# A decoder-layer kernel: one PSUM bank taken from the spread of B and given to the common set

## What is computed

```python
x = x + attn(layernorm(x))            # 16 heads of 32; chunked linear attention with feature maps, rms norm per head
x = x + mixer(ctx, layernorm(x))      # selective scan over 512 steps, 512 channels, 16 states; gate silu(z)
x = x + ffn(layernorm(x))             # 512 -> 2048 gate and value, ternary weights, 8-bit activations, -> 512

# mixer, the part that the change touches
dA = exp(d[..., None] * A)
state = state * dA + (d * u)[..., None] * b[:, None, :]
y = einsum('bdn,bn->bd', state, c)
```

## Time and profile before

| | us |
|---|---|
| median of 3 runs (lowest, highest) | 1216.23 (1215.35, 1216.56) |
| the profiled execution, its own time | 1215.45 |
| its span, first to last instruction | 1213.7 |
| busy: TensorE / VectorE / ScalarE / GpSimd | 893.5 / 928.2 / 585.0 / 435.6 |
| mean granted TensorE clock | 0.821 of full |

### The profile page before, as it was taken

One profiled execution on the slowest core, in us unless ns is written; L12 is line 12 of the kernel. 1 busy time (PEld: TensorE's weight loads), 2 busy tenths in 40 slices (PEclk: granted clock), 3 DMA queues, 4 the chain that ended last, 5 costly groups with the idle time before them and its releaser, 6 DMA issues.

```text
span 1213.7 us, 11854 instructions
## 1 busy us (share of the span) xinstructions
PE 893.5 (74%) x3970; PEld 487.3 (40%) x3970; DVE 928.2 (76%) x1065; ACT 585.0 (48%) x887; POOL 435.6 (36%) x264
## 2 busy tenths in 40 slices
PE   4576765636628989978628989978628999976597
PEld 1334333414222346555222446555222356743233
DVE  4878889999897676888798676988798668853453
ACT  2787426345435763453435763454435754321332
POOL 0134554344345332534245332534245334540100
PEclk8688686655958999985958999985958999967699
DMA  9368778776535533646335533646335435740000
GB/s 323 109 185 237 171 191 227 176 190 188 115 81 120 124 76 72 159 91 154 82 79 121 122 77 71 158 95 153 82 80 112 114 87 130 168 93 0 1 9 26
DMA packets 57120, 147.20 MB, mean 121 GB/s; under 512 B 7938, under 2 KB 8322, under 8 KB 57060
## 3 DMA queue, kind: packets, MB, share of 16 engines
q0 software_dynamic: 18432, 67.12, 28.8%
q1 hardware_dynamic: 38628, 79.32, 20.9%
HBM read 74.96 MB, written 4.35 MB: 65 GB/s over the span
## 4 chain that ended last, share of the span: by engine, by line
PE 43%; DVE 27%; DMA 14%; issue 7%; ACT 6%; POOL 1%; SPq 0%; DVEq 0%; POOLq 0%; ACTq 0%
PE bank L586 16%; DMA ACC<-W 14%; PE bank L750 7%; DVE W L1381 7%; PE bank L615 4%; DVE W L1372 4%; PE bank L766 3%; PE bank L665 3%; PE bank L634 3%; PE bank L747 2%; PE bank L686 2%; DVE BST L1308 2%; DVE U L1331 2%; DVE X L1529 1%; POOL W L1235 1%
## 5 line engine op out<-in xcount | busy, mean ns | idle before, releaser
L1235 POOL TENSOR_TENSOR W<-W,CROW 128x1024 f32<-128x1024 f32 x128 | 310.7, 2427 | 473.4 <-DVE W L1381 473.3
L1381 DVE TENSOR_TENSOR_SCAN W<-DEC,W 128x1024 f32<-128x1024 f32 x122 | 306.3, 2511 | 0.1
L1243 POOL DMA_DIRECT2D ACC<-W x128 | 115.0, 898 | 178.5 <-DMA ACC<-W 152.6
L1372 DVE TENSOR_TENSOR W<-DU,PB 128x1024 f32<-128x1024 f32 x128 | 153.1, 1196 | 21.5 <-PE PB L712 11.3
L948 ACT ACTIVATE DEC<-DT,ACOL 128x511 f32<-128x511 f32 x244 | 160.0, 712 | 5.7 <-DVE W L1381 5.6
L750 PE MATMUL bank<-W,ARENA 128*128 128x512 fp8e4 x512 | 144.1, 408 | 0.0
L615 PE MATMUL bank<-IDF,ARENA 128*128 128x128 f32 x400 | 64.8, 311 | 82.5 <-DVE ARENA L1549 53.3
L895 ACT ACTIVATE ARENA<-bank 128x512 f32<-128x512 f32 x56 | 33.1, 592 | 157.4 <-PE bank L634 80.2
L1470 DVE SCALAR_TENSOR_TENSOR ARENA<-bank,SDQ,ARENA 128x512 f32<-128x512 f32 x64 | 47.6, 747 | 79.3 <-PE bank L750 50.8
L615 PEld LDWEIGHTS bank<-IDF,ARENA 128*128 128x128 f32 x400 | 54.4, 162 | 104.8 <-issue 90.0
L1019 ACT ACTIVATE ARENA<-bank,SDQ 128x512 f32<-128x512 f32 x64 | 43.5, 685 | 80.4 <-PE bank L750 80.3
(11 more groups left out here) (158 smaller groups left out, 1466.3 us busy)
## 6 DMA issues: line engine op xcount, KB each, us to landing
ACC<-W POOLq DMA_DIRECT2D x128, 512.0 KB, 5.6
CROW<-c_rows SPq DMA_DIRECT2D x128, 256.0 KB, 3.5
W<-in_wffn SPq DMA_DIRECT2D x27, 512.0 KB, 7.2
X<-in_wffn SPq DMA_DIRECT2D x21, 512.0 KB, 5.7
X<-in_x SPq DMA_DIRECT2D x7, 1024.0 KB, 9.3
out_dram<-X SPq DMA_DIRECT2D x16, 256.0 KB, 2.1
X<-in_ctxT SPq DMA_DIRECT2D x4, 512.0 KB, 4.7
ARENA<-in_x SPq DMA_DIRECT2D x1, 1024.0 KB, 5.6
```

The costliest lines, as they stand in the source:

```text
L1235: pool.tensor_tensor(w, w, CROW[u % 2][:, :].unsqueeze(1).broadcast_to([P, 2, L]), ALU.mult)\
L1243: pool.dma_start(ACC[accumulator(u)][:, :, :], w, accum_op=ALU.add).then_inc(y_summed.sem, 16)
L1372: dve.tensor_tensor(W[u % 4][:, :, :], DU[:, 2 * h:2 * h + 2, :], PB[u % 3][:, :].unsqueeze(1).broadcast_to([P, 2, L]), ALU.mult)\
L1381: dve.tensor_tensor_scan(w, flat(decay_of(u)), w, 0.0, ALU.mult, ALU.add).then_inc(scan_done.sem, 1)
```

## The change

One bank moves from PB to the common set; PSUM's eight banks are all in use before and after. The diff, cut to its core:

```diff
-    every, four, last = (0, 1, 2, 3, 4), (0, 1, 2, 3), (4,)
+    every, five, last = (0, 1, 2, 3, 4, 5), (0, 1, 2, 3, 4), (5,)
...
-        return [(key, last if key[1] == "o" else four) for key in attention_products(b)]
+        return [(key, last if key[1] == "o" else five) for key in attention_products(b)]
...
-        out += on((0, 1, 4) if b < BATCH else every, [(f, "yT", t) for t in range(TT)])
+        out += on((0, 1, 4, 5) if b < BATCH else every, [(f, "yT", t) for t in range(TT)])
...
-        R = Banks(ctx, nc, "bank", 5, all_products())
-        PB = [ctx.enter_context(nc.psum_tensor(f"PB{i}", [P, 512], fp32)) for i in range(3)]
+        R = Banks(ctx, nc, "bank", 6, all_products())
+        PB = [ctx.enter_context(nc.psum_tensor(f"PB{i}", [P, 512], fp32)) for i in range(2)]
...
-                if u >= 3:
-                    pe.wait_ge(*dbu_done.at(0, u - 2))
+                if u >= 2:
+                    pe.wait_ge(*dbu_done.at(0, u - 1))
...
-                pe.matmul(PB[u % 3][:, :], ID96[:, n:n + 1].broadcast_to([96, P]), BC3[b % 2][:, :],
+                pe.matmul(PB[u % 2][:, :], ID96[:, n:n + 1].broadcast_to([96, P]), BC3[b % 2][:, :],
...
-                                  PB[u % 3][:, :].unsqueeze(1).broadcast_to([P, 2, L]), ALU.mult)\
+                                  PB[u % 2][:, :].unsqueeze(1).broadcast_to([P, 2, L]), ALU.mult)\
```

More of the change, by code:

```diff
@@ L171, in attention @@
     def attention(b):
-        return [(key, last if key[1] == "o" else four) for key in attention_products(b)]
+        return [(key, last if key[1] == "o" else five) for key in attention_products(b)]
     out = on(every, front_products(0) + [(0, "dt", e) for e in range(KT)] + [(0, "xnT", k) for k in range(KT)])
-    out += on(four, [(0, "q", 0), (0, "k", 0), (0, "v", 0)] + front_products(1))
+    out += on(five, [(0, "q", 0), (0, "k", 0), (0, "v", 0)] + front_products(1))
     out += attention(0)
@@ L178, in all_products @@
         f = b - 1
-        out += on(four, [(f, "ms", GROUPS - 1)])
+        out += on(five, [(f, "ms", GROUPS - 1)])
         if b < BATCH:
-            out += on(four, [(b, "dt", 2), (b, "dt", 3)] + [(b, "xnT", k) for k in range(KT)])
+            out += on(five, [(b, "dt", 2), (b, "dt", 3)] + [(b, "xnT", k) for k in range(KT)])
         out += on(every, [(f, "wo", t) for t in range(TT)])
@@ L191, in all_products @@
         if b < BATCH:
-            out += on(four, [(b, "v", 0)])
+            out += on(five, [(b, "v", 0)])
         out += on(every, [(f, "O", TT - 1)])
```

## The result

The changed kernel is slower. Its median is **1221.48 us** (11 runs, 1217.73 to 1224.42) against 1215.78 us (11 runs, 1212.93 to 1218.05) for the kernel before on the same chip. The ratio is 1.0046, 95% interval 1.0033 to 1.0059: 5.6 us by the ratio, 5.7 by the medians. The profiled execution took 1222.39 us, its span is 1220.6 us, 6.9 more than that of before, its mean granted clock 0.822.

A forecast was written before the change was run, and what follows sets the result against it. No engine bounds the kernel alone (chain: TensorE 43%, VectorE 27%, accumulating DMA 14%). Terms 1.3 + 0 + 2.1 + 0.2 = +3.6 us on the profiled 1215.45 give 1219.05, plus 0.78 for the median: 1219.8, range 1215.3 to 1227.0.

The forecast's parts named there:

- Place 1: Row 0's start: the spread of unit 2 waits for `inputs_b(0)` and delays q; +1.3 us (0.6 to 1.9).
- Place 2: Row 0's attention: unit 17's spread runs 5.0 us later, covered by VectorE's 3.66 us DMA wait; 0 (0 to 2.7).
- the worse of its two cases: Row 0's attention, group 1: k as slow as before, VectorE 4.2 us late; at full clock 1.6 us.
- Place 3: Three feed-forwards beside units: the clock falls after the new stop; +0.7 us each, +2.1 in all (-1.2 to +6.6).
- Place 4: Last attention group of rows 1 and 2: unit 63's spread waits some 4 us; +0.2 us for both (0 to 1.0).
- Gained, 0: Bank waits elsewhere than in the feed-forward are 1 us or less, or end in a data wait: nothing gained.
- Not slower: the stops are free: Row 0's start costs 0.6 us, TensorE keeps full clock in the feed-forward: -0.6 us, about 1215.6 to 1217; chance 0.25.
- More half clock: Row 0's start, feed-forwards and last attention groups at their upper ends: +9.5 us, 1225.7; chance 0.20.
- Faster: the freed bank wins outright: Feed-forward without bank wait or clock fall: hT 5.4 us earlier, three times 16.2, 1201.3; chance 0.05.

The follow-up runs named there:

- the first experiment: The kernel before with two spread banks instead of three, the common set kept at five and the eighth bank unused: 1223.82 us, ratio 1.0068.
- the one with both moves: The changed kernel with unit 2's spread issued behind q and k, and three spreads of each feed-forward beside units issued later: 1204.80 us, ratio 0.9921.

## Why the prediction was right, and where its terms were off

The forecast was +3.6 us and 1219.8; the medians give +5.7 and 1221.48, inside the range, slower as the likeliest case. The mechanism holds: the tighter wait costs time where TensorE is on the path, through TensorE's clock, and most of it has cover. The terms don't all hold, and that the sum came this near is in part luck:

- **The reading of the earlier trace rows was wrong.** "19 of 128 spreads, 27.2 us in all" counts weight loads and matmuls of the same spreads. It was 13 spreads, and 10.5 us of stops between matmuls. The conclusion drawn from it, that a tighter limit bites there, stands; no term of the sum uses the figure.
- **Place 1, +1.3 (0.6 to 1.9): too small in the profiled execution, right in others.** The later start of q was as worked out, 1.9 us. What failed in the profiled execution is "if the clock rises at the same moment as before, part of the slow stretch is spent waiting". The clock rose later too: 0.58 in 55 to 60 where before had 0.98, q took 6.50 us. 2.7 us at conv, above the upper end. In three other kernels with two banks and the start as in after, whose executions began otherwise, the step held, and the loss at conv was 0.7 to 1.3 us. Nor does all of it last: of after's delay 1.1 us was left when the first feed-forward began.
- **Place 2, 0 (0 to 2.7): right.** The k product was slow (5.92 us), as in the worse of its two cases; VectorE came 5.8 us late to the scores, 3.1 of them new (4.2 were worked out, where its own numbers give 4.1), and left the group 2.4 us late, less than the 2.7 that it had come with. The wait of 3.66 us for the DMA was the cover and is gone.
- **Place 3, +0.7 each, +2.1 in all: too small.** Measured +1.8, +2.1 and +2.0, 5.9 in all, near the upper end of +2.2 each. The step that failed is that I took the new stop before the second spread for the one that brings the clock down. The stop before the first spread, 2.70 us, already did. Four to five products at 2.35 us followed, and not two or three. The second stop, worked out as 3.1 us, was then 0.74. The added matmuls show that the clock is the price: with the waits kept and the clock full the same stretch is 1.0 to 1.3 us quicker than before.
- The Trainium skill's rule that I weighed there ("TensorE: Matmul & The Clock Gate", section "A second HAM failure mode: psum-queue depth-cycling") pointed the right way: the granted clock was 0.50 and 0.52 in the thirteen microseconds behind 381 where before had 1.00 and 0.64, and filling the stop held it at 1.00. Of the upper ends that I had tied to it, this place came near its own and place 1 went past it at conv; places 2 and 4 stayed low.
- **Place 4, +0.2: right.** The transposes behind the last spread of row 1's attention are still released by VectorE's `feature` step, after a wait of 0.36 us (554.91). From the end of one feed-forward to the start of the next VectorE's delay even fell, by 0.5 us over row 1, 0.6 over row 2 and 2.4 over row 3. There the half clock lies elsewhere, as one window of the last groups of row 3's attention shows (0.81 and 1.00), of before and then of after:

```profile
1060.00:1080.00 20.00, 15.68 (x97) 10.84 (x96) 16.14 (x15) 6.81 (x11) 10.62 (x7) 0.81 0.61 122
```

```profile
1060.00:1080.00 20.00, 17.70 (x113) 11.81 (x114) 15.41 (x17) 8.34 (x14) 10.18 (x7) 1.00 0.62 132
```

- **Gained, 0: not settled.** The waits for banks other than the earlier trace rows were read as "1 us or less, or end in a wait for data". One of them is 1.50 us, before "xin" 3, and it went. The freed bank by itself gave some 2.7 us by the ratios of after and of the first experiment, within their intervals. Against it stand the two slow xdbl, 5.3 us and not 3.6, on the path: +1.7 and +2.0 us, which no term has. That the freed bank makes them slow is not shown: with "xin" 3 held back both stay slow, and with five banks the one of row 1 is slow as well.
- VectorE's delay in the profiled execution adds up as follows: 1.1 when the first feed-forward began, 5.9 in the three steps, 4.0 at the ends of the three feed-forwards (1.7, 2.0, 0.4), less 3.4 between them, and 0.5 in the last part: +8.1. The prediction had 1.3 for the first, 2.1 for the second, nothing for the ends and +0.2 for what lies between. What it missed at the ends and what came back between them nearly cancel, and nothing in it foresaw either.

**The rivals.** "Not slower: the stops are free" fell; its point was whether matmuls behind the stop take 1.3 us a product, and they took 2.35. "More half clock" is what happened in the feed-forward; its sum of +9.5 was not reached, in the profiled execution because of the time that came back between the feed-forwards. "Faster: the freed bank wins outright" did not happen, but its mechanism and price are real: 5.4 us a feed-forward were worked out, and -4.8 to -5.1 measured in before with other placements, -4.0 to -4.9 in the changed kernel with the spreads moved and V placed. What kept it from happening is what the prediction named, `inputs_b` of the unit before, and a second thing that it had not seen: V had no bank either.

## What to carry to other kernels

A buffer taken from an in-order queue's most frequent product costs little in waiting (88 us more of stops here, and almost all covered) and more in what the waiting does to TensorE's clock: look at what the granted clock is behind each new stop and price the products after it at that level. A wait for a bank is a statement on one product and the one that stood in its bank: before adding a bank at another's cost, look at whom it waits for and put it where something is drained early; here three placements gave 12 us, where the extra bank alone gave some 2.7 within the noise, and 5.6 once the spreads were out of its way. A total that a view gives for a line can hold a weight load and its matmul: look at them apart before you price a stop. Where a limit must be tighter, move the instruction that waits behind those that don't.

## What the runs showed of the chip

- A stop of TensorE of 2.70 us was followed by the half clock (0.50 in 381 to 388) in after, as one of 3.29 us was in before; stops of 1.06 and 0.50 us between stretches of matmuls were followed by 1.00. A stop of 2.44 us before the same product was followed by a fall in two of six cases (the kernel with the feed-forward spreads moved) and by 1.00 in the other four (one more of that kernel, three of the one with both moves).
- Twenty matmuls with no reader in each of three feed-forwards, 60 in all, went with a mean granted clock of 0.834 to 0.852 (eight executions) where it had been 0.816 to 0.824 (six), and brought the median down from 1223.82 to 1208.94 us.
- The same instructions at the same place ran at either level in different executions and kernels (xdbl 3.6 or 5.3 us), so a place's price on the clock is not the same in each row of a batch. In row 0 q took 6.4 to 6.5 or 5.0 to 5.1 us behind the same wait.
